# A graph network on one core: the merge of an item's rows moves into the next step

## The chip, the cores and the metric

The kernel runs on one core of one Trainium2 chip. The metric is the device time of one execution in microseconds (us); the time of a kernel is the median of several executions.

## What is computed

A graph has 6250 nodes and 206250 edges sorted by destination node. Three attention layers (GATv2) run over it, then a layer norm, then a node model that uses sums of the edge attributes, then another layer norm. Cut to what matters here, one layer is:

```python
e_feat = leaky_relu(xl[src] + xr[dst])            # xl = h @ Wl + bl, xr = h @ Wr + br
logits = einsum('ehc,hc->eh', e_feat, att)
m      = segment_max(logits, dst)                 # per destination node and head
a      = exp(logits - m[dst]); denom = segment_sum(a, dst)
h      = segment_sum(xl[src] * a / denom[dst], dst) + bias
h      = relu(layer_norm(h) * g + be)             # input of the next layer
```

The node model also needs `segment_sum(edge_attr, dst)` and a count per node; the kernel takes both in its first layer.

## The kernel before, in words

Edges are cut into chunks of 3328 (26 tiles of 128), and a chunk with its window of 128 destination nodes is an **item**: 62 items in each of three **stages** (one stage per attention layer). All engines run the same software pipeline, written out by hand in `pipeline` (L450) as a chain of **steps**. A step *opens* one item, *closes* the item opened a step earlier, and *begins* the next one (its preparation). In stages 0 and 1 it also *turns* an item closed earlier: it makes that window's rows of the next layer's tables.

The 26 tiles are handled in 7 groups, six of four tiles and one of two. For an opened item, per group:

- GpSimd gathers the rows `xl[src]` by one indirect DMA per tile (L706). It may be two groups ahead of VectorE and no more: before group g it waits for the z of group g-2 (L701), and for groups 0 and 1 for the last two groups of the item before (L703).
- ScalarE builds one-hot matrices: `S` (edge by node, `onehot`, L906 and L909) and its transpose `ST` (`onehotT`, L931 and L936).
- TensorE spreads the node rows `xr` over the edges with `ST` (`expand`, L763; groups 0 and 1 of an item are made at the end of the step before, L812).
- VectorE adds both parts, which is z (`add_transforms`, L1186), and takes the logits (`relu_att` L1193, `sum_heads` L1202 or L1205, `add_linear` L1216).

For a closed item VectorE finds the running maxima over segments (`runs`, `carries`, `maxima`), subtracts them (`shift`, L1275), ScalarE takes the exponentials (L953), VectorE weights the gathered rows (`message`, L1285), and TensorE sums them by node into one PSUM bank (`sums`, L791; in stage 0 also the edge attributes, `attribute_sums`, L783, with a clearing product L778 ahead). Then comes the **merge** with the state of that window in memory: `new_max` (L1294 to L1304), an exponential on ScalarE (`rescale`, L966), `new_state` (L1311 to L1320). In stages 0 and 1 `turn_norm` (L1328 to L1344, 15 dependent small operations) normalizes the merged rows; TensorE transposes and multiplies them (`turn_rows` L743, `turn_products` L748 and L749), ScalarE copies (L885, L894, L896), VectorE takes their logits (`turn_logits`, L1352 to L1361).

In the kernel before, VectorE does `new_max` in the last group of the step that closes the item, and `new_state` and `turn_norm` behind that group, at the end of the step. The next step begins with `runs`, and only then comes its first z. SyncE loads items and stores rows in a fixed order (`item_step`, L605): it waits for the merge, stores the window, waits for the store, and loads the next window.

Each engine runs its own list in order, so a waiting instruction holds everything behind it.

## Time and profile before

| | |
|---|---|
| median of 3 executions | 8529.99 us (8517.47 to 8535.05) |
| the profiled execution | 8491.84 us, span 8489.9 us |
| busy: TensorE, VectorE, ScalarE, GpSimd | 4879.8, 5222.4, 4307.0, 4740.8 us |
| mean granted TensorE clock | 0.679 of full speed |
| moved by DMA | 697.83 MB, mean 82 GB/s |

The profiled execution is 0.45% below the median. The span runs from the first to the last instruction. No engine is busy for more than 62% of it.

### The profile page before, as it was taken

To read this page: it belongs to the slowest core of one execution; us is meant where nothing else is said; L and a number is where in the kernel's file an instruction comes from. 1 tells how busy PE (TensorE), PEld (TensorE's weight loads), DVE (VectorE), ACT (ScalarE), POOL (GpSimd) and SP (SyncE) were. 2 spreads that over 40 slices of the span, in tenths; PEclk is the share of its full clock that TensorE was granted. 3 is DMA by queue.
4 is the path that set the end of the run, shared out by engine and by line. 5 is a ranking of instruction groups with operands and counts; after the bars stand their busy time and mean duration, and the time that the engine had idled before them with its cause. 6 is when DMAs were issued, how large, how long until landed. Compare 5 with 4: busy or idle time off the path is not lost.

```text
span 8489.9 us, 109176 instructions
## 1 busy us (share of the span) xinstructions
PE 4879.8 (57%) x24176; PEld 4286.7 (50%) x24176; DVE 5222.4 (62%) x16308; ACT 4307.0 (51%) x10681; POOL 4740.8 (56%) x4843
## 2 busy tenths in 40 slices
PE   4666666666666655555555555545555555544446
PEld 3565656565656544444444444444444444444444
DVE  5555565656565656766666667655555555555556
ACT  3444444444454545555555555545555555555546
POOL 3555555555555545666666666656666666666640
PEclk7666666666666666766767767666666666666666
DMA  5333333333333322322322323222222222222221
GB/s 147 94 100 91 96 97 97 97 96 97 96 98 95 98 67 74 79 76 76 77 75 77 82 77 78 76 66 72 77 71 71 72 72 72 76 73 72 72 61 50
DMA packets 460163, 697.83 MB, mean 82 GB/s; under 512 B 140781, under 2 KB 330019, under 8 KB 460101
## 3 DMA queue, kind: packets, MB, share of 16 engines
q0 software_dynamic: 154752, 327.15, 16.9%
q1 hardware_dynamic: 305349, 370.00, 14.2%
q8 instruction: 21, 0.34, 0.0%
q14 instruction: 41, 0.34, 0.0%
HBM read 638.95 MB, written 57.76 MB: 82 GB/s over the span
## 4 chain that ended last, share of the span: by engine, by line
PE 33%; issue 27%; DVE 22%; another core or an unknown queue 7%; ACT 6%; POOL 3%; DMA 2%; SPq 0%; DVEq 0%; ACTq 0%; POOLq 0%
PE PS L791 14%; PE PS L763 10%; PE PS L783 6%; DVE z L1186 3%; POOL xl_g L706 3%; DVE am L1193 3%; DVE msg L1285 2%; ACT distT L931 2%; ACT ST L936 2%; DVE relu_logit L1202 1%; ACT dist L906 1%; PE PS L749 1%; DMA xl_g<-xl_tab,edges 1%; DVE relu_logit L1205 1%
## 5 line engine op out<-in xcount | busy, mean ns | idle before, releaser
L706 POOL DMA_INDIRECT xl_g<-xl_tab,edges x4836 | 4740.0, 980 | 3485.8 <-DVE z L1186 1689.1
L763 PE MATMUL PS<-xr_w,ST 128*128 128x132 f32 x9672 | 2054.2, 373 | 2160.7 <-issue 1278.8
L763 PEld LDWEIGHTS PS<-xr_w,ST 128*128 128x128 f32 x9672 | 1778.9, 269 | 2455.4 <-issue 1735.2
L791 PE MATMUL PS<-msg,S 128*128 128x137 f32 x9672 | 1829.7, 352 | 936.8 <-issue 648.7
L791 PEld LDWEIGHTS PS<-msg,S 128*128 128x128 f32 x9672 | 1710.6, 257 | 1017.6 <-issue 1012.0
L1186 DVE TENSOR_TENSOR z<-PS,xl_g 128x528 f32<-128x528 f32 x1302 | 856.6, 658 | 1428.1 <-DMA xl_g<-xl_tab,edges 823.2
L906 ACT ACTIVATE dist<-node_row,neg_dst 128x128 f32<-128x128 f32 x4836 | 1534.5, 386 | 0.0
L931 ACT ACTIVATE distT<-dst_all,neg_node 128x512 f32<-128x512 int16 x1302 | 884.0, 679 | 1029.7 <-DVE neg_dst L1179 725.5
L909 ACT ACTIVATE S<-dist 128x512 f32<-128x512 f32 x1302 | 780.4, 599 | 839.9 <-remote 625.2
L1193 DVE SCALAR_TENSOR_TENSOR am<-z,att_relu 128x512 f32<-128x512 f32 x1302 | 860.8, 661 | 115.0 <-remote 94.1
L936 ACT ACTIVATE ST<-distT 128x512 f32<-128x512 f32 x1302 | 780.0, 599 | 42.6 <-ACT distT L931 1.4
L1285 DVE TENSOR_TENSOR msg<-xl_g,msg 128x512 f32<-128x512 f32 x1302 | 792.8, 644 | 0.2 <-ACT msg L953 0.2
L783 PE MATMUL PS<-ea,S 128*128 128x96 f32 x3224 | 628.6, 366 | 194.3 <-issue 194.1
L783 PEld LDWEIGHTS PS<-ea,S 128*128 128x128 f32 x3224 | 593.1, 278 | 260.3 <-issue 260.0
L1202 DVE TENSOR_REDUCE relu_logit<-am 128x16 f32<-128x512 f32 x868 | 557.0, 642 | 30.6 <-DVE am L1193 11.1
L1294 DVE TENSOR_SCALAR some<-PS 128x1 f32<-128x1 f32 x186 | 29.5, 158 | 836.2 <-PE PS L791 578.2
L966 ACT ACTIVATE rescale<-dmax 128x8 f32<-128x8 f32 x186 | 38.8, 208 | 879.0 <-DVE dmax L1304 802.1
L953 ACT ACTIVATE msg<-shifted 128x104 f32<-128x104 f32 x186 | 56.7, 305 | 716.0 <-issue 522.7
L1205 DVE TENSOR_REDUCE relu_logit<-am 128x4 f32<-128x512 f32 x434 | 278.3, 641 | 22.7 <-DVE am L1193 11.9
L1216 DVE TENSOR_TENSOR logit<-relu_logit,z 128x16 f32<-128x16 f32 x1302 | 227.5, 175 | 93.0 <-remote 82.1
L1243 DVE TENSOR_TENSOR_SCAN run_up<-row_pen,PS 128x128 f32<-128x128 f32 x186 | 77.8, 418 | 175.0 <-PE PS L770 98.7
L894 ACT COPY t_lr<-PS 128x264 f32<-128x264 f32 x124 | 46.9, 378 | 246.1 <-PE PS L749 168.7
(220 smaller groups left out, 3691.4 us busy)
## 6 DMA issues: line engine op xcount, KB each, us to landing
dst_all<-dst_short SPq DMA_DIRECT2D x186, 832.0 KB
xl_g<-xl_tab,edges POOLq DMA_INDIRECT x4836
ea<-edge_attr SPq DMA_DIRECT2D x124, 432.0 KB
ea<-edge_attr SPq DMA_DIRECT2D x62, 384.0 KB
xr_w<-xr_tab SPq DMA_DIRECT2D x186, 66.0 KB
dst_r<-dst_rows SPq DMA_DIRECT2D x186, 64.0 KB
node_row<-node_id SPq DMA_DIRECT2D x186, 64.0 KB
state<-t_new SPq DMA_DIRECT2D x126, 68.0 KB
```

What stands on the lines that cost most here:

```text
L706: pool.indirect_dma_start(xl_g[:, q, t, :], None, xl_tab[stage][:, :], bass.IndirectOffsetOnAxis(idx[:, q, t:t + 1], 0))\
L763: last = pe.matmul(zp[(q + g) % 3][:, n, :], ST[:, t, :], xr_w[:, q, :], start=True, stop=True)
L783: last = pe.matmul(ea_ps, S[:, q, t, :], ea[:, q, t, :], start=False, stop=False)
L791: last = pe.matmul(agg_ps, S[:, q, t, :], msg[:, t, :], start=t == 0 and stage > 0, stop=t == TILES - 1)
L906: last = act.activation(dist[:, (q + g) % 2, m, :], node_row[:, q, :], ACT.Abs, bias=neg_dst[:, q, t:t + 1])
L909: act.activation(S[:, q, GROUPS[g][0]:GROUPS[g][0] + n, :], dist[:, (q + g) % 2, 0:n, :], ACT.Relu, bias=1.0, scale=-1.0)\
L931: act.activation(distT[:, (q + g) % 2, 0:n], dst_all[:, q, GROUPS[g][0] * P:GROUPS[g][0] * P + n], ACT.Abs, bias=neg_node[:, q:q + 1]).the ...
L936: act.activation(ST[:, GROUPS[g][0]:GROUPS[g][-1] + 1, :].rearrange("p t n -> p (t n)"), distT[:, (q + g) % 2, 0:n], ACT.Relu, bias=1.0, s ...
L1186: dve.tensor_tensor(out=z[:, (q + g) % 2, 0:n, :], in0=zp[(q + g) % 3][:, 0:n, :], in1=xl_g[:, q, a:a + n, :], op=ALU.add).then_inc(z_done ...
L1193: dve.scalar_tensor_tensor(am[:, (q + g) % 2, 0:n, :], z[:, (q + g) % 2, 0:n, 0:F], 0.0, att_relu[:, stage, :].unsqueeze(1).to_broadcast([ ...
L1202: s = dve.reduce_sum(relu_logit[:, a * HEADS:(a + n) * HEADS], am[:, (q + g) % 2, 0:n, :].rearrange("p t (h f) -> p (t h) f", h=HEADS), ax ...
L1285: dve.tensor_tensor(out=msg[:, a:a + n, 0:F].rearrange("p t (h f) -> p t h f", h=HEADS), in0=xl_g[:, q, a:a + n, 0:F].rearrange("p t (h f) ...
```

## The change

The argument `turned` of a step becomes `merges`: the item that was closed one step earlier, in all three stages (the last stage gets one more step at its end for that). Merge and normalization of an item now run in the step after the one that closes it:

- VectorE: a step begins with the z of group 0, then `new_max` of the item merged, then `runs` of the item closed. `new_state` stands behind the z of group 1, `turn_norm` at the end of group 1, `turn_logits` in group 5 (it was in group 2).
- ScalarE: `rescale` stands behind the first one-hot of the step; the two turning copies and the exponentials of the closed item trade places.
- TensorE: `turn_rows` and `turn_products` go from groups 0 and 1 to groups 2 and 3. Ahead of the sums TensorE waits, as before, for the copy that frees the bank, and in the last stage for the merge (`item_done`).
- SyncE: the state of item k-1 is stored, and that of item k loaded, behind the loads for item k+2; the turned rows are stored behind the attribute loads.

```diff
                     for g in range(NG):
                         if opens and g + 2 < NG:
                             expand(opens, g + 2)
-                        if turned and g < 2:
-                            (turn_rows, turn_products)[g]()
                         if closes and g == 2:
                             close("max")
+                        if turned and g in (2, 3):
+                            (turn_rows, turn_products)[g - 2]()
                         if turned and closes and g == 3:
                             pe.wait_ge(n_copied, turned[1] + BLOCKS)
+                        elif merges and closes and g == 3:
+                            pe.wait_ge(item_done, merges[1])
...
                     if opens:
                         onehotT(opens, 2)
+                    if merges:
+                        rescales()
+                    if opens:
                         onehot(0)
+                        onehotT(opens, 3)
+                        onehot(1)
+                        onehotT(opens, 4)
                     if turned:
                         turn_hidden()
+                    if closes:
+                        alphas()
                     if opens:
-                        onehotT(opens, 3)
-                        onehot(1)
+                        onehotT(opens, 5)
+                        onehot(2)
                     if turned:
                         turn_copies()
...
                 for g in range(NG):
-                    if closes and g == 0:
-                        runs()
-                    if closes and g == 1:
-                        carries()
                     if opens:
                         add_transforms(g)
                         if g:
                             add_linear(g - 1)
+                    if merges and g == 1:
+                        new_state()
+                    if closes and g == 1:
+                        carries()
                     if closes and g == 2:
                         shift()
-                    if turned and g == 2:
+                    if turned and g == 5:
                         turn_logits()
                     if opens:
                         relu_att(g)
+                    if merges and g == 0:
+                        new_max()
...
                         sum_heads(g)
-                    if closes and g == NG - 1:
-                        new_max()
+                    if closes and g == 0:
+                        runs()
+                    if turned and g == 1:
+                        turn_norm()
...
                 if opens:
                     add_linear(NG - 1)
-                if closes:
-                    new_state()
-                    if stage < LAYERS - 1:
-                        turn_norm()
...
                 def item_step(k, q, behind):
-                    here, ahead = window(k), window(k + 1)
...
                     load_item(k + 2, q, stage)
-                    if turns and behind:
-                        store_turned(k - 1, stage, before)
+                    if behind:
+                        store_merged(k, q)
...
+                    if turns and behind:
+                        store_turned(k - 1, stage, before)
```

**VectorE, the head of a step in stage 0, before.** `t_norm` ends the normalization; `run_up` and `run_down` are `runs`; `z`, `am`, `relu_logit` are group 0.

```order
L1344 TENSOR_SCALAR t_norm<-t_y,t_mv,t_rstd 128x128
L1243 SCALAR_TENSOR_TENSOR run_up<-row_pen,PS 128x128
L1244 SCALAR_TENSOR_TENSOR run_down<-row_pen,PS 128x128
L1186 TENSOR_TENSOR z<-PS,xl_g 128x528
L1193 SCALAR_TENSOR_TENSOR am<-z,att_relu 128x512
L1202 TENSOR_REDUCE relu_logit<-am 128x16
L1251 STREAM_TRANSPOSE run_T<-run_up 128x32
```

The same place now, from the z of group 0 to the z of group 1; `some` to `dmax` is `new_max`.

```order
L1205 TENSOR_TENSOR z<-PS,xl_g 128x528
L1212 SCALAR_TENSOR_TENSOR am<-z,att_relu 128x512
L1313 TENSOR_SCALAR some<-PS 128x1
L1315 TENSOR_SCALAR none_pen<-some 128x1
L1317 TENSOR_SCALAR chunk_max<-PS,none_pen 128x4
L1320 TENSOR_TENSOR st_new<-chunk_max,st_old 128x4
L1322 TENSOR_TENSOR dmax<-st_old,st_new 128x4
L1323 TENSOR_TENSOR dmax<-chunk_max,st_new 128x4
L1221 TENSOR_REDUCE relu_logit<-am 128x16
L1262 SCALAR_TENSOR_TENSOR run_up<-row_pen,PS 128x128
L1263 SCALAR_TENSOR_TENSOR run_down<-row_pen,PS 128x128
L1205 TENSOR_TENSOR z<-PS,xl_g 128x528
```

The z of group 0 now stands ahead of the merge and of `runs`.

**VectorE, ahead of the z of group 2 in stage 0, before** (`up` and `seg_max` are `maxima`, `shifted` is `shift`):

```order
L1267 SCALAR_TENSOR_TENSOR up<-row_pen,carry_T,PS 128x128
L1269 SCALAR_TENSOR_TENSOR seg_max<-row_pen,carry_T,up 128x128
L1202 TENSOR_REDUCE relu_logit<-am 128x16
L1186 TENSOR_TENSOR z<-PS,xl_g 128x528
L1216 TENSOR_TENSOR logit<-relu_logit,z 128x4x4
L1275 TENSOR_TENSOR shifted<-logit,PS 128x104
```

And now, with the last operations of `turn_norm` ahead of it:

```order
L1361 SCALAR_TENSOR_TENSOR t_newton<-t_rstd,t_half 128x1
L1362 SCALAR_TENSOR_TENSOR t_rstd<-t_newton,t_rstd 128x1
L1363 TENSOR_SCALAR t_norm<-t_y,t_mv,t_rstd 128x128
L1205 TENSOR_TENSOR z<-PS,xl_g 128x528
L1235 TENSOR_TENSOR logit<-relu_logit,z 128x4x4
L1294 TENSOR_TENSOR shifted<-logit,PS 128x104
```

The whole normalization has moved from ahead of the first z to ahead of the third.

**TensorE, a step of stage 0 from the transposed logits (`L770`) to the first attribute sums (`L783`), before:**

```order
L770 MATMUL PS<-ident,logit 128x128
L763 MATMUL PS<-xr_w,ST 128x132 x4
L743 MATMUL PS<-ident,t_norm 128x128
L763 MATMUL PS<-xr_w,ST 128x132 x4
L748 MATMUL PS<-b_parts,ones_h 128x264
L749 MATMUL PS<-w_lr,t_hT 128x264
L763 MATMUL PS<-xr_w,ST 128x132 x4
L773 MATMUL PS<-ident,seg_max 128x128
L763 MATMUL PS<-xr_w,ST 128x132 x4
L778 MATMUL PS<-zeros,ones 128x233
L783 MATMUL PS<-ea,S 128x96 x9
```

And now:

```order
L774 MATMUL PS<-ident,logit 128x128
L767 MATMUL PS<-xr_w,ST 128x132 x12
L777 MATMUL PS<-ident,seg_max 128x128
L747 MATMUL PS<-ident,t_norm 128x128
L767 MATMUL PS<-xr_w,ST 128x132 x4
L752 MATMUL PS<-b_parts,ones_h 128x264
L753 MATMUL PS<-w_lr,t_hT 128x264
L782 MATMUL PS<-zeros,ones 128x233
L787 MATMUL PS<-ea,S 128x96 x9
```

The two turning products now stand directly ahead of the sums.

## Rows read from the trace of the kernel before

**Rows 1.** The page: busy us (share of the span) and instructions of each engine
```profile
PE 4879.8 (57%) x24176; PEld 4286.7 (50%) x24176; DVE 5222.4 (62%) x16308; ACT 4307.0 (51%) x10681; POOL 4740.8 (56%) x4843
```
**Rows 2.** Line L1294 in stage 0, 1 and 2: duration ns, first and last start
```profile
L1294 DVE TENSOR_SCALAR some<-PS x62: 157/158/160, 194.1 to 3065.6; 128x1 f32<-128x1 f32 x62
...
L1294 DVE TENSOR_SCALAR some<-PS x62: 157/159/160, 3165.0 to 5668.9; 128x1 f32<-128x1 f32 x62
...
L1294 DVE TENSOR_SCALAR some<-PS x62: 157/159/160, 5767.0 to 8249.4; 128x1 f32<-128x1 f32 x62
```
**Rows 3.** Timeline, VectorE, a stage 0 step: start us, us, operation [idle before <-releaser]
```profile
2003.31 0.16 DVE L1294 TENSOR_SCALAR some<-PS 128x1 f32<-128x1 f32 x1 [9.63 <-PE PS L791]
...
2004.75 0.29 DVE L1311 TENSOR_TENSOR scaled<-st_old,rescale 128x128 f32<-128x128 f32 x1 [0.19 <-ACT rescale L966]
...
2005.85 0.18 DVE L1328 RECIPROCAL t_rd<-st_new 128x4 f32<-128x4 f32 x1
...
2009.74 0.41 DVE L1243 TENSOR_TENSOR_SCAN run_up<-row_pen,PS 128x128 f32<-128x128 f32 x1
...
2010.38 0.68 DVE L1186 TENSOR_TENSOR z<-PS,xl_g 128x528 f32<-128x528 f32 x1
...
2015.97 0.65 DVE L1202 TENSOR_REDUCE relu_logit<-am 128x16 f32<-128x512 f32 x1
...
2028.22 0.71 DVE L1186 TENSOR_TENSOR z<-PS,xl_g 128x528 f32<-128x528 f32 x1 [0.81 <-DMA xl_g<-xl_tab,edges]
...
2056.94 0.68 DVE L1186 TENSOR_TENSOR z<-PS,xl_g 128x528 f32<-128x528 f32 x1
```
**Rows 4.** Timeline, TensorE, the same step
```profile
2014.16 0.40 PE L748 MATMUL PS<-b_parts,ones_h 3*128 3x264 bf16 x1
...
2024.22 2.13 PE L763 MATMUL PS<-xr_w,ST 128*128 128x132 f32 x8 [3.85 <-issue]
...
2027.35 4.16 PE L783 MATMUL PS<-ea,S 128*128 128x96 f32 x18
...
2049.40 0.80 PE L763 MATMUL PS<-xr_w,ST 128*128 128x132 f32 x5 [0.19 <-issue]
```
**Rows 5.** Timeline, ScalarE, the same step
```profile
2015.99 0.38 ACT L894 COPY t_lr<-PS 128x264 f32<-128x264 f32 x1 [2.18 <-PE PS L749]
...
2022.80 0.70 ACT L931 ACTIVATE distT<-dst_all,neg_node 128x512 f32<-128x512 int16 x1
```
**Rows 6.** Timeline, GpSimd, the same step
```profile
2011.85 0.94 POOL L706 DMA_INDIRECT xl_g<-xl_tab,edges  x1 [13.65 <-DVE z L1186]
```
**Rows 7.** Line L706, GpSimd, whole span: duration ns min/median/max
```profile
L706 POOL DMA_INDIRECT xl_g<-xl_tab,edges x4836: 938/944/1487, 102.4 to 8226.3; - x194
```
**Rows 8.** Timeline, VectorE, a stage 1 step
```profile
4513.68 0.71 DVE L1186 TENSOR_TENSOR z<-PS,xl_g 128x528 f32<-128x528 f32 x1 [2.34 <-issue]
...
4514.85 0.28 DVE L1352 TENSOR_TENSOR t_sum<-t_lr 128x128 f32<-128x128 f32 x1
...
4516.09 0.69 DVE L1193 SCALAR_TENSOR_TENSOR am<-z,att_relu 128x512 f32<-128x512 f32 x1
...
4528.70 0.71 DVE L1186 TENSOR_TENSOR z<-PS,xl_g 128x528 f32<-128x528 f32 x1 [0.63 <-DMA xl_g<-xl_tab,edges]
...
4532.04 0.69 DVE L1193 SCALAR_TENSOR_TENSOR am<-z,att_relu 128x512 f32<-128x512 f32 x1 [2.54 <-remote]
...
4534.30 0.43 DVE L1186 TENSOR_TENSOR z<-PS,xl_g 128x264 f32<-128x264 f32 x1
```
**Rows 9.** Timeline, ScalarE, the same stage 1 step
```profile
4514.80 0.30 ACT L953 ACTIVATE msg<-shifted 128x104 f32<-128x104 f32 x1 [2.18 <-issue]
```
**Rows 10.** Timeline, TensorE, the same stage 1 step
```profile
4536.82 1.17 PE L763 MATMUL PS<-xr_w,ST 128*128 128x132 f32 x8 [0.81 <-issue]
```
**Rows 11.** Timeline, a stage 2 step: GpSimd, then VectorE
```profile
7011.61 0.94 POOL L706 DMA_INDIRECT xl_g<-xl_tab,edges  x1 [4.34 <-DVE z L1186]
...
7042.90 0.43 DVE L1186 TENSOR_TENSOR z<-PS,xl_g 128x264 f32<-128x264 f32 x1 [5.75 <-remote]
```

More of the change, by code:

```diff
@@ L455, in item @@
                 return q, pairs * (2 * stage) + 2 * i + (q + 1), pairs * stage + i + 1
-            def turned(i, q):
-                return item(i, q) if stage < LAYERS - 1 else None
             step(None, None, item(0, 0), None)
@@ L603, in _, with store_merged, logits_made @@
                 sp.dma_start(st_old[:, 0, 0:ROW if first else ROW_L], state[stage][bass.ds(windows[0], P), :]).then_inc(state_loaded[0], 16)
-                def item_step(k, q, behind):
-                    here, ahead = window(k), window(k + 1)
+                width = ROW if first else ROW_L
+                def store_merged(k, q):
+                    here, ahead = window(k - 1), window(k)
+                    sp.sem_inc(spacer, 1)
+                    sp.wait_ge(item_done, before + k)
+                    sp.dma_start(state[stage][bass.ds(here, P), :], st_new[:, 1 - q, 0:width]).then_inc(state_stored, 16)
+                    sp.wait_ge(state_stored, (before + k) * 16)
+                    sp.dma_start(st_old[:, q, 0:width], state[stage][bass.ds(ahead, P), :]).then_inc(state_loaded[q], 16)
+                def logits_made(k):
                     sp.wait_ge(onehot_done[NG - 1], (before + k + 1) * 2)
@@ L736, in _, with pe_step @@
             for stage in range(LAYERS):
-                def pe_step(opens, closes, begins, turned):
+                def pe_step(opens, closes, begins, merges):
+                    turned = merges if stage < LAYERS - 1 else None
                     def turn_rows():
@@ L879, in _, with act_step @@
             for stage in range(LAYERS):
-                def act_step(opens, closes, begins, turned):
+                def act_step(opens, closes, begins, merges):
+                    turned = merges if stage < LAYERS - 1 else None
                     def turn_hidden():
@@ L1042, in _ @@
             ch = Chain(dve, setup)
+            dve.sem_inc(merge_step, 4)
             for g in range(NG):
@@ L1170, in node_logits, with edge_step @@
                 assert n.n == LOGIT_STEPS, n.n
-            def edge_step(stage, opens, closes, begins, turned):
+            def edge_step(stage, opens, closes, begins, merges):
+                turned = merges if stage < LAYERS - 1 else None
                 def prepare():
@@ L1417, in _ @@
             for stage in range(LAYERS):
-                pipeline(dve, stage, pairs, last_pair, lambda opens, closes, begins, turned: edge_step(stage, opens, closes, begins, turned))
+                pipeline(dve, stage, pairs, last_pair, lambda opens, closes, begins, merges: edge_step(stage, opens, closes, begins, merges))
             dve.wait_ge(hid_bias, 1)
```

85 lines of the change are left out of this document (38 added, 47 removed).

## The prediction

> **What bounds the kernel now.** I read the page first. No engine is near its span: VectorE is busy 5222.4 us of 8489.9, GpSimd 4740.8, TensorE 4879.8 [rows 1]. So the time is not an engine's work but a loop of waits. Next, the line that opens the merge, stage by stage. It runs 62 times in each, so 61 steps lie between its first and last start [rows 2]: (3065.6-194.1)/61 = 47.1 us a step in stage 0, 41.05 in stage 1, 40.7 in stage 2. That makes 61 x 128.8 = 7860 of the 8490 us; the rest is set-up, stage ends and the node model, which the change leaves alone.
>
> Then the timeline of one step of stage 0. The merge starts at 2003.31, after VectorE stood idle 9.63 us for TensorE's sums; merge, normalization and `runs` take until 2010.38, and only there stands the first z [rows 3]. GpSimd, which may gather only two groups ahead of z, had been idle 13.65 us and starts 0.8 us behind that z [rows 6]. Everything later in the step follows from it. In stage 0 TensorE starts its long run of sums at 2027.35 and is through with it and with the spread of the next item's group 0 at 2049.40+0.80 = 2050.20 [rows 4]. The next z comes at 2056.94 [rows 3]. So the loop is: z, sums start (17.0 us later), sums and spread end (22.85), merge chain until the next z (6.7): 46.6 us, close to the mean of 47.1. In stages 1 and 2 the same loop holds, with the gathers as its middle part: the GpSimd waits there are 4.34 us in the stage 2 step shown [rows 11].
>
> **The change, part by part.** It adds and removes next to no work: the same operations on other places. What counts is what each place holds up.
>
> *(a) The first z no longer waits for merge, normalization and `runs`.* It still waits for the spread of group 0, which TensorE, in order, does behind the sums. In stage 0 it can come 0.15 us behind 2050.20 in place of 2056.94: -6.6 us a step.
>
> *(b) The same VectorE work now lies between z of group 0 and z of group 2.* Before, from z at 2010.38 to the end of the group 1 reduction at 2015.97+0.65, VectorE ran without a gap: 6.2 us. To it comes 2003.31 to 2010.38, 7.07 us, less 0.19 of waiting and 0.17 for the last group's `add_linear` that lies inside [rows 3]: 6.7. So z of group 2 can start 12.9 us behind the first z. (Without the normalization, 2005.85 to 2009.74, it is 9.0.)
>
> *(c) The turning products now stand right ahead of the sums.* From z of group 2: exponentials done after 4514.80+0.20-4513.68 = 1.3 us [rows 8, 9]; the transposed one-hot of group 5, 2022.80 to TensorE's start at 2024.22, 1.4 [rows 4, 5]; its spread, 2.1; the two products and the copy, 2014.16 to 2015.99+0.38, 2.2 [rows 4, 5]; then 1.0 from the end of the spread at 2026.35 to the first attribute sum, with the clearing product [rows 4]. 12.9+1.3+1.4+2.1+2.2+1.0 = 20.9, with hand-overs 21.0, against 17.0: +4.0 us a step in stage 0.
>
> *Stage 0*: 21.0+22.85+0.15 = 44.0 against 46.56: -2.5 us. x 61 = **-153 us**. ScalarE's last S one-hots, now behind the copy, are covered by the 22.85 us of sums, which begin with attributes.
>
> *Stage 1*, no attribute sums, so the gathers set the middle. GpSimd may start group 4 when z of group 2 is done: 12.9+0.7+0.8 = 14.4. In the stage 0 step group 4's z came at 2028.22, 16.4 us behind GpSimd's start of group 2 at 2011.85 [rows 3, 6], less two groups of four at 0.944+0.30 us each [rows 7] (10.0): 6.4 from a group's start to its z. One group later, +5.1: z of group 5 at 25.9. To z of group 6, 4534.30-4528.70 = 5.6, plus `turn_logits`, which moved in there, 1.25 (4514.85 to 4516.09): 6.85 [rows 8]. From there to the next first z: one-hot and spread of group 0, which began 4536.82-4534.30 = 2.5 later and took 1.2 [rows 8, 10], and I take 0.5 for sums still ahead of it on TensorE: 4.2. Sum 37.0; the shown steps are shorter than the mean (46.6 against 47.1), so 37.8 against 41.05: -3.2 us. x 61 = **-195 us**.
>
> *Stage 2*, no normalization: z of group 2 at 9.0 is not late for the gathers. GpSimd's wait for the first z, 4.34 us, shrinks to the usual 0.30 [rows 11]: -4.0. Against that stands contention. With two SBUF operands on VectorE beside them, gathers grew from 0.944 to as much as 1.487 us [rows 7]; the merge has some four such operations that used to run while GpSimd waited. Between nothing and 4 x 0.54 = 2.2 I take 0.3, since the mean gather is near its median. -3.7 x 61 = **-226 us**.
>
> On that point the Trainium skill, "GPSIMD Engine Reference", section 1 (Specifications), says that GpSimd shares its SBUF interfaces with VectorE and contends with VectorE instructions that have two SBUF inputs. The rule speaks against this change; by it at its full price stage 2 would gain 1.8 us a step in place of 3.7. The trace agrees that some gathers are longer, up to 1.487 us, and does not say by which operation.
>
> *SyncE*: the item loads no longer wait for the merge in stages 1 and 2, so their burst comes some 3 us earlier and may meet the gathers of groups 0 and 1. No row shows it there; bounds 0 and +2 us a step, taken as 0, since in the stage 1 step, with the burst right ahead of it, VectorE waited no more than 2.34 us for the gather of group 2 [rows 8]. State store and load have a whole step of slack: nothing. *Stage ends*: the last merge waited for the last sums before and does so now: nothing, at worst 5 us each.
>
> Sum: -574 us. The profiled execution of 8491.8 becomes 7918; it stood 0.45% below the median of 8530, so the forecast is **7950 us**.
>
> **The rivals.**
>
> *R1, faster than forecast.* Late in a step all engines stand still without a releaser that the trace names: 2.54 us in the stage 1 step [rows 8], 5.75 us in the stage 2 step [rows 11]. I carried these over. If they belong to the old arrangement, stages 1 and 2 come down to the gathers' floor: 26 x 1.3+0.8 = 34.6 in stage 2 (-6.1), 35.6 in stage 1 (-5.4), and stage 0, where TensorE's sums hold such a stall too, to -5.2. That is -1020 us: 7510. For it: nothing in the program asks for the stalls. Against: they stand in nearly every step.
>
> *R2, a third of the gain.* Burst and contention at their upper ends (+2 and +1.9 a step in stages 1 and 2), stage 0 -1.5: -1.5, -1.2, -1: some -225 us, 8300.
>
> *R3, slower.* TensorE takes its list in order. In stages 0 and 1 it now holds sums, and behind them the next item's spread and so the next first z, until ScalarE's copy of the turned rows is done; that copy was 11 us early before (2016.37 against 2027.35 [rows 4, 5]) and is the last thing to come now. It decides once the copy comes 4.7 us later than 19.9 us behind the first z (574/122 steps). If a late-step stall (up to 5.75 us) falls ahead of it, both stages lose: 122 x 5.75-574 = +128 us, 8660. For it: the products run on a TensorE that has just waited. Against: the stall shown stood behind the z of group 5 [rows 8], not ahead.
>
> *R4, it doesn't do what it says.* If the first z waits for something else by the same amount (the gather of group 0, say), (a) is empty and (b), (c) nearly so: 8530. Against: GpSimd had stood idle for 13.65 us ahead of its group 2 [rows 6], so groups 0 and 1 had long been issued.
>
> **How the numbers follow.** Forecast 0.56, R1 0.17, R2 0.17, R3 0.06, R4 0.04. Cases that leave the range: half of R1's far end, R3, R4. The range is 7580 to 8370 us. A measurement tells 0.2%, some 17 us, from no change: faster 0.90, within 0.03, slower 0.07.
>
> **What would show it.** Right: L1313 of the new profile spaced 44 to 45 us in stage 0, about 38 in stage 1, 37 in stage 2; GpSimd's long idle ahead of group 2 gone and, in stages 0 and 1, a shorter one ahead of group 4; z of group 2 some 13 us behind the first z, 9 in stage 2; the first attribute sum 21 us behind it, released by the copy L902. Wrong: a step of stage 0 over 47 us; TensorE waiting for L902 past 25 us; steps of stage 1 or 2 under 36 us, which would be R1; GpSimd's mean gather over 1.05 us, which would be R2.

## The result and the profile after

| | before | changed | ratio, 95% interval |
|---|---|---|---|
| the timed pair | 8529.99 us | 8574.09 us (8559.03 to 8581.07) | 1.0058 [1.0046, 1.0069] |
| the same pair again, in a later session (e7) | 8473.16 us | 8301.36 us (8286.34 to 8309.03) | 0.9799 [0.9781, 0.9816] |

The change made the kernel 0.6% slower where 6.8% faster was forecast. Run again in another session it was 2% faster. (A session, named a call in the expectations below, stands for kernels timed together on one chip, beside fresh runs of before. The five later sessions each had another chip; that of the first pair is not on record.) So there are two questions: why the gain is small everywhere, and why its sign changes.

The line that opens the merge, stage by stage, first timed pair, changed kernel (against [rows 2]):

```profile
L1313 DVE TENSOR_SCALAR some<-PS x62: 150/151/159, 200.3 to 2974.9; 128x1 f32<-128x1 f32 x62
...
L1313 DVE TENSOR_SCALAR some<-PS x62: 150/151/159, 3082.4 to 5741.0; 128x1 f32<-128x1 f32 x62
...
L1313 DVE TENSOR_SCALAR some<-PS x62: 150/152/159, 5848.6 to 8317.2; 128x1 f32<-128x1 f32 x62
```

Divided by 61: 45.5, 43.6 and 40.5 us a step, against 47.1, 41.05 and 40.7. Stage 0 gained 97 us, stage 1 lost 155, stage 2 gained 14, and what lies between and around the stages cost 23: +67 us, the difference of the spans (8557.0 and 8489.9). So the loss is in stage 1. One of its steps, all engines, in order of time (start us, us, operation, idle before and releaser):

```profile
4537.25 0.71 DVE L1205 TENSOR_TENSOR z<-PS,xl_g 128x528 f32<-128x528 f32 x1 [7.82 <-PE PS L767]
...
4551.17 0.70 DVE L1205 TENSOR_TENSOR z<-PS,xl_g 128x528 f32<-128x528 f32 x1
...
4552.68 1.10 POOL L708 DMA_INDIRECT xl_g<-xl_tab,edges  x1 [3.80 <-DVE z L1205]
...
4558.35 2.16 PE L795 MATMUL PS<-msg,S 128*128 128x137 f32 x8 [0.88 <-issue]
...
4567.89 1.02 DVE L1304 TENSOR_TENSOR msg<-xl_g,msg 128x512 f32<-128x512 f32 x2
...
4568.71 0.72 PE L795 MATMUL PS<-msg,S 128*128 128x137 f32 x4 [0.83 <-issue]
4568.82 0.42 DVE L1205 TENSOR_TENSOR z<-PS,xl_g 128x264 f32<-128x264 f32 x1
...
4571.97 0.28 PE L795 MATMUL PS<-msg,S 128*128 128x137 f32 x1 [2.54 <-issue]
...
4572.68 0.42 DVE L1221 TENSOR_REDUCE relu_logit<-am 128x8 f32<-128x256 f32 x1 [2.18 <-issue]
...
4574.78 0.39 PE L795 MATMUL PS<-msg,S 128*128 128x137 f32 x1 [2.53 <-issue]
4574.80 0.72 ACT L939 ACTIVATE distT<-dst_all,neg_node 128x512 f32<-128x512 int16 x1 [8.04 <-remote]
4575.15 0.94 POOL L708 DMA_INDIRECT xl_g<-xl_tab,edges  x1 [0.30 <-issue]
...
4576.88 0.39 PE L795 MATMUL PS<-msg,S 128*128 128x137 f32 x1 [1.71 <-issue]
...
4578.30 1.49 PE L795 MATMUL PS<-msg,S 128*128 128x137 f32 x5 [1.04 <-issue]
...
4581.59 0.71 DVE L1205 TENSOR_TENSOR z<-PS,xl_g 128x528 f32<-128x528 f32 x1 [5.22 <-PE PS L767]
```

z of group 2 comes 13.9 us behind the first z (forecast 12.9), z of group 6 31.6 us behind it (32.8). Up to here it is within 1.2 us of the forecast. But from there to the next first z it takes 12.8 us, where 4.2 were forecast. The last messages are there at 4568.9; TensorE then does its last sums one by one with 1 to 2.5 us between them, and VectorE and ScalarE stand still beside it. GpSimd alone keeps its pace. Its chain of 18 indirect DMAs began at 4552.68 (the longest pause in it is 0.67 us), TensorE stops some 17 us into it, the last DMA of the step ends at 4576.09, and 2 us later everybody runs again.

TensorE's weight loads stand still as well. By their event records the two that start at 4573.38 and 4576.17 neither wait for a semaphore nor update one:

```profile
4573.38 0.29 PEld L795 LDWEIGHTS PS<-msg,S 128*128 128x128 f32 x1 [2.65 <-issue]
4576.17 0.29 PEld L795 LDWEIGHTS PS<-msg,S 128*128 128x128 f32 x1 [2.50 <-issue]
```

The stall was there before, in the stage 1 step of [rows 8]. GpSimd's chain of 18 began at 4506.64 and ended at 4529.53; ScalarE stops 17 us into it, between `dist` operations that are done and the `S` that needs nothing else:

```profile
4506.64 0.94 POOL L706 DMA_INDIRECT xl_g<-xl_tab,edges  x1 [4.06 <-DVE z L1186]
...
4526.44 0.63 ACT L909 ACTIVATE S<-dist 128x512 f32<-128x512 f32 x1 [2.56 <-remote]
```

VectorE's 2.54 us of [rows 8] end 2.5 us behind that chain. So it is this late-step stall, grown. In all of stage 1, TensorE's idle time in front of the sums:

```profile
L795 PE MATMUL PS<-msg,S 128*128 128x137 f32 x3172 | 665.9, 369 | 549.4 <-issue 546.5 <-ACT t_lr L902 1.7 <-DVE msg L1304 1.0
```

That is 546.5/61 = 9.0 us a step in which it waited for nothing that the trace names. Some 0.9 of them stand at the first sum (4558.35), which follows ScalarE's copy L902 (done at 4558.11), and are no stall.

One more thing changed beside it: the mean granted TensorE clock of stage 1 was 0.69 before and 0.63 now, and TensorE's busy time a step rose from 22.6 to 24.6 us. The mean sum took 369 ns in both. How much of the 2.0 us lies on the path was not tested.

### The profile page after: what moved, and what is told of

Read it like the earlier page. It is cut to its first block, busy times and chain, and to the rows that moved or that the text cites. A ratio compares the mean times of both kernels' runs of the same rounds, so it can differ in the third digit from the quotient of the medians.

```text
span 8557.0 us, 109590 instructions
## 1 busy us (share of the span) xinstructions
PE 4961.6 (58%) x24176; PEld 4337.0 (51%) x24176; DVE 5109.9 (60%) x16308; ACT 4305.5 (50%) x10681; POOL 4791.0 (56%) x4843
## 4 chain that ended last, share of the span: by engine, by line
PE 33%; DVE 30%; issue 23%; another core or an unknown queue 8%; ACT 4%; DMA 1%; POOL 1%; DVEq 1%; SPq 0%; ACTq 0%; POOLq 0%
PE PS L795 16%; PE PS L767 7%; PE PS L787 6%; DVE z L1205 5%; DVE am L1212 3%; DVE msg L1304 2%; PE PS L753 2%; ACT distT L939 1%; DVE t_newton L1361 1%; ACT ST L944 1%; DVE t_bits L1358 1%; DVE relu_logit L1221 1%; DVE t_rstd L1362 1%; DVE relu_logit L1224 1%
## 5 line engine op out<-in xcount | busy, mean ns | idle before, releaser
L708 POOL DMA_INDIRECT xl_g<-xl_tab,edges x4836 | 4790.2, 991 | 3506.1 <-issue 1774.1
L767 PE MATMUL PS<-xr_w,ST 128*128 128x132 f32 x9672 | 2144.0, 389 | 1945.3 <-ACT ST L944 1099.4
L767 PEld LDWEIGHTS PS<-xr_w,ST 128*128 128x128 f32 x9672 | 1886.6, 285 | 2175.0 <-issue 1605.0
L795 PE MATMUL PS<-msg,S 128*128 128x137 f32 x9672 | 1850.7, 351 | 1016.8 <-issue 949.5
L1212 DVE SCALAR_TENSOR_TENSOR am<-z,att_relu 128x512 f32<-128x512 f32 x1302 | 841.0, 646 | 10.0 <-DVE z L1205 2.3
L787 PE MATMUL PS<-ea,S 128*128 128x96 f32 x3224 | 548.0, 339 | 39.5 <-issue 39.2
L787 PEld LDWEIGHTS PS<-ea,S 128*128 128x128 f32 x3224 | 528.3, 255 | 58.5 <-issue 58.1
L893 ACT ACTIVATE t_hT<-PS,be_col,g_col 128x128 f32<-128x128 f32 x124 | 56.7, 457 | 737.2 <-PE PS L747 737.2
L747 PE MATMUL PS<-ident,t_norm 128*128 128x128 f32 x124 | 59.0, 475 | 380.6 <-DVE t_norm L1363 380.6
L1294 DVE TENSOR_TENSOR shifted<-logit,PS 128x104 f32<-128x104 f32 x186 | 60.5, 325 | 316.3 <-remote 298.7
```

Of the source, the lines that this page charges most:

```text
L708: pool.indirect_dma_start(xl_g[:, q, t, :], None, xl_tab[stage][:, :], bass.IndirectOffsetOnAxis(idx[:, q, t:t + 1], 0))\
L767: last = pe.matmul(zp[(q + g) % 3][:, n, :], ST[:, t, :], xr_w[:, q, :], start=True, stop=True)
L787: last = pe.matmul(ea_ps, S[:, q, t, :], ea[:, q, t, :], start=False, stop=False)
L795: last = pe.matmul(agg_ps, S[:, q, t, :], msg[:, t, :], start=t == 0 and stage > 0, stop=t == TILES - 1)
L1212: dve.scalar_tensor_tensor(am[:, (q + g) % 2, 0:n, :], z[:, (q + g) % 2, 0:n, 0:F], 0.0, att_relu[:, stage, :].unsqueeze(1).to_broadcast([ ...
```

## The experiments

"Us a step" is the spacing of the merge's first line. The expectations count from z to z in the middle of a stage, which gives some 0.5 us more (44.2 where the table has 43.6). For stage 1, "sum gaps" is the idle time in front of the sums by issue, as in the row above. The kernels of the first four later sessions (e1 to e4, e5 to e8, e9 to e12, e13 to e16) ran beside runs of before at 8459 to 8475 us, those of the last (e17, e18) at 8521. Where one execution alone was taken, its time stands in place of a ratio.

| kernel | us a step, stages 0, 1, 2 | sum gaps, us a step | ratio |
|---|---|---|---|
| before, first trace | 47.1, 41.05, 40.7 | | 1 |
| changed, first trace | 45.5, 43.6, 40.5 | 9.0 | 1.0058 |
| e12 before | 46.8, 40.7, 40.7 | 2.5, and 3.1 remote | 1 |
| e7 changed | 44.0, 41.8, 39.6 | 8.3 | 0.980 |
| e1 half the gathers | 44.0, 31.4, 28.6 | 0 | 6917 us |
| e2 small item load | 44.0, 42.0, 39.8 | 8.3 | 8323 us |
| e5 narrow rows | 43.9, 41.8, 39.9 | 8.6 | 8314 us |
| e6 plain DMAs | 44.05, 31.1, 28.0 | 0 | 6866 us |
| e9 pause for z of group 6 | 42.9, 45.4, 40.3 | 0.9 | 1.001 |
| e10 pause for the sums | 44.0, 46.2, 39.9 | 0.9 | 8590 us |
| e13 pauses ahead of groups 2, 4, 6 | 43.7, 41.3, 41.1 | 0.3 | 0.985 |
| e14 before, same pauses | 43.6, 41.85, 41.7 | 2.7 | 0.990 |
| e15 pause ahead of each | 48.2, 47.9, 48.3 | | 9506 us |
| e16 64 more instructions | 46.9, 46.6, 47.45 | 4.4 | 9247 us |
| e3 spread first | 44.7, 41.5, 40.2 | | 0.987 |
| e4 change in stage 0 | 44.05, 40.6, 40.9 | | 0.9815 |
| e8 the same, spread first | 44.5, 40.6, 40.7 | | 0.984 |
| e11 change in stages 0 and 2 | 44.0, 40.7, 40.3 | | 0.971 |
| e17 two pauses | 44.3, 43.4, 39.9 | | 0.990 |
| e18 e11 and e9's wait in stage 0 | 44.2, 41.3, 40.3 | | 0.980 |

**What the stall needs: e1, e2, e5, e6.**

```diff
-for t in tiles:
+for t in tiles[::2] if stage else tiles:
```


> The changed kernel, but in stages 1 and 2 only every second tile of a group is gathered (13 indirect DMAs an item in place of 26); VectorE works on old rows for the others, so this part of the computation is left out there. Stage 0 is unchanged. In the changed kernel a step of stage 1 takes 44.2 us, and between 32 and 42 us behind its first z TensorE does single sums with 1 to 2.5 us between them though its operands are ready: 7 to 9 us a step. Theory G (the stall comes from GpSimd's gathers when they run without a pause): the gaps in the sums shrink below 2 us a step and stage 1 falls to 35 us or less. Theory L (the stall comes from the item load): gaps stay at 7 us, a step takes about 42 us. Theory I (instruction supply that has nothing to do with either): also stays. My forecast's own sum, with no gathers in the way, gives about 33 us for stage 1.

```diff
-dst_all[:, q, :], dst_short[bass.ds(ch, 1), :]
+dst_all[:, q, 0:wide], dst_short[bass.ds(ch, 1), 0:wide]     # wide = P if stage else CHUNK
```


> The changed kernel, but in stages 1 and 2 the broadcast of an item's destinations to all partitions loads 128 columns in place of 3328 (0.03 MB in place of 0.85 MB); the one-hots there use old destinations, so this part of the computation is left out. Theory L (the item load causes the late stall): gaps in the sums of stage 1 fall from 8 to under 2 us, a step from 44.2 to about 37. Theory G and theory I: stage 1 stays at 43 to 44.5 us, the gaps at 7 us or more.

```diff
-pool.indirect_dma_start(xl_g[:, q, t, :], None, xl_tab[stage][:, :], ...)
+pool.indirect_dma_start(xl_g[:, q, t, 0:wide], None, rows[:, :], ...)     # wide = 33 in stages 1 and 2
```


> The changed kernel, but in stages 1 and 2 each of the 26 indirect DMAs of an item fetches 33 numbers a row in place of 132: as many DMAs and rows, a quarter of the bytes; rows are other ones and the rest of each row is old, so this part is left out. With half the DMAs (e1) the stall was gone and a step of stage 1 took 31.6 us. If the bytes matter (the transfer engines are the shared resource): the stall goes, stage 1 takes 35 to 38 us, the gathers' floor. If the number of rows and GpSimd's work on them matter: the stall stays, stage 1 at 42 to 44 us.

```diff
+else:
+    pool.dma_start(xl_g[:, q, t, :], xl_tab[stage][t * P:(t + 1) * P, :]).then_inc(gathered[q][g], 16)
```


> The changed kernel, but in stages 1 and 2 GpSimd fetches each tile by a plain DMA of 128 consecutive rows in place of an indirect one: as many DMAs and the same bytes, no indices; rows are other ones, so this part is left out. If what stalls the engines is GpSimd's work on the indices: the stall goes, stage 1 takes 34 to 37 us or less. If it is the transfers or the number of DMAs: stage 1 stays at 42 to 44 us.

The sums in stage 1 of e1, e2, e5 and e6, each from its own trace (busy us, mean ns, idle before):

```profile
L795 PE MATMUL PS<-msg,S 128*128 128x137 f32 x3172 | 544.0, 344 | 53.2 <-ACT t_lr L902 53.2
```
```profile
L796 PE MATMUL PS<-msg,S 128*128 128x137 f32 x3172 | 639.6, 360 | 515.8 <-issue 503.9 <-ACT t_lr L903 8.7 <-DVE msg L1305 2.1
```
```profile
L796 PE MATMUL PS<-msg,S 128*128 128x137 f32 x3171 | 647.1, 364 | 541.3 <-issue 526.0 <-ACT t_lr L903 11.3 <-DVE msg L1305 3.6
```
```profile
L798 PE MATMUL PS<-msg,S 128*128 128x137 f32 x3172 | 538.3, 341 | 53.1 <-ACT t_lr L905 53.1
```

A twenty-sixth of the load's columns and a quarter of the gathers' bytes change nothing: theory L and the bytes are out. Half the indirect DMAs, or plain DMAs of the same bytes, take the gaps to zero and a step of stage 1 to 31 us. So the stall of the three other engines comes with GpSimd's indirect DMAs at their full rate. Whether plain DMAs could bring it on is open: e6's occupy GpSimd for 535 ns in place of 944, and no chain of them was longer than 10, or 6.1 us. e1's longest was 5 us.

**How they do it: e9, e10, e13, e15.**

```diff
-pool.wait_ge(z_done[NG + g - BEHIND], ...)
+pool.wait_ge(z_done[NG - 1], ...)
```


> The changed kernel, in which GpSimd waits ahead of groups 0 and 1 of the next item for the z of the last group (it waited for that of the last but one for group 0): a pause of some 4 us in the chain of indirect DMAs of a step, nothing else. e1 and e6 showed that the stall of the other engines comes with the indirect DMAs, at a full rate for 17 us or more. If a pause lets the others recover: the gaps in the sums of stage 1 (8 us a step) fall to 3 us or less, the first z is then held by the gather of group 0, some 41 us behind the last first z, and stage 1 goes from 42.3 to 41 or less; ratio 0.5 to 1% under the changed kernel's 0.980. If the number of indirect DMAs in a step decides: no change in the gaps, the later gathers only add, ratio 0.980 to 0.99.

Both branches of that were wrong for stage 1. The gaps did leave the sums (the 0.9 us that are left are the wait for the copy), yet the step grew to 45.4 us. VectorE in a stage 1 step of e9:

```profile
4164.28 0.18 DVE L1235 TENSOR_TENSOR logit<-relu_logit,z 128x16 f32<-128x16 f32 x1
...
4167.02 0.21 DVE L1273 TENSOR_TENSOR_SCAN open_max<-through_pen,run_T 128x26 f32<-128x26 f32 x1 [1.49 <-issue]
...
4169.83 0.19 DVE L1277 TENSOR_TENSOR carry<-open_max,enter_pen 128x26 f32<-128x26 f32 x1 [2.50 <-remote]
...
4172.62 0.25 DVE L1280 STREAM_TRANSPOSE carry_T<-carry 128x64 f32<-128x64 f32 x1 [2.50 <-issue]
```

and GpSimd, where the chain starts and where it ends:

```profile
4151.44 0.95 POOL L708 DMA_INDIRECT xl_g<-xl_tab,edges  x1 [4.58 <-DVE z L1205]
...
4160.20 0.95 POOL L708 DMA_INDIRECT xl_g<-xl_tab,edges  x1 [0.30 <-issue]
...
4170.27 0.94 POOL L708 DMA_INDIRECT xl_g<-xl_tab,edges  x1 [0.30 <-issue]
```

The later gathers of groups 0 and 1 now run into those of groups 2 and 3 without a pause, 16 DMAs or 20 us, and the stall stands 14 us into that chain, on small VectorE operations that need nothing from DMA. In the changed kernel's step above it stood some 17 us behind 4552.68. The stall goes with the chain, not with the place in the program. In stage 0 e9's pauses break the chain, and a step fell from 44.0 to 42.9 us.

```diff
+if stage == 1 and g == 0:
+    pool.wait_ge(agg_done, ...)     # the last sums of the item being closed
```


> The changed kernel, but in stage 1 GpSimd starts the gathers of the next item only when TensorE has done the last sums of the item being closed, so that no indirect DMA runs beside the end of the sums. If the stall needs indirect DMAs beside the stalled work: no gaps in the last sums, which end some 33 us behind the first z (40 in e7); the next first z then waits for a gather, 33+8 = 41 us. If the stall is owed to what went before in the step (a store that has run empty, say), the gaps stay and a step of stage 1 takes 48 us or more.

As e9: the long gaps in the sums are gone, and the stall stands in `carries`, 16 to 20 us into a chain of 16 (46.2 us a step). Step and gaps together fit neither branch: the first had left out where the stall would go.

```diff
+if g in PAUSES:     # (2, 4, 6); each of 1 to 6 in e15
+    pool.wait_ge(gathered[q][g - 1], (pairs * stage + i + 1) * (16 * len(GROUPS[g - 1])))
```


> The changed kernel, in which GpSimd waits ahead of groups 2, 4 and 6 until the rows of the group before have landed (some 2 us each). No unbroken chain of indirect DMAs is then longer than 10 (12.6 us; it was 18 or more, 23 us and over). As many DMAs as before. If an unbroken chain of some 16 us is what brings the stall: no gaps in the sums of stage 1, which is then held by GpSimd at 26 x 1.25+3 x 2 = 38.5 to 39.5 us (42.3), stage 2 at 38.5 to 39 (40.2), stage 0 at 43.3 (44.4): 250 to 370 us less than the changed kernel, ratio 0.936 to 0.951. If the number of DMAs decides: the pauses only cost, 0.98 to 1.01.

> As e13, with a pause ahead of each of groups 1 to 6, so that no chain is longer than 6. If chains of 10 are short enough, there is nothing left to win and the pauses cost: 26 x 1.25+6 x 2 = 44.5 us a step in stages 1 and 2, and no stall in any. If a stall was left in e13 and is gone here, the chain must be shorter than 10.

The sums of stage 1 in e13:

```profile
L799 PE MATMUL PS<-msg,S 128*128 128x137 f32 x3172 | 623.1, 368 | 257.7 <-DVE msg L1308 188.4 <-ACT t_lr L906 49.0 <-issue 20.3
```

and GpSimd's pauses in one of its steps:

```profile
4090.95 0.94 POOL L712 DMA_INDIRECT xl_g<-xl_tab,edges  x1 [2.58 <-issue]
...
4103.69 1.35 POOL L712 DMA_INDIRECT xl_g<-xl_tab,edges  x1 [2.58 <-DMA xl_g<-xl_tab,edges]
...
4116.65 0.94 POOL L712 DMA_INDIRECT xl_g<-xl_tab,edges  x1 [2.56 <-DMA xl_g<-xl_tab,edges]
```

As many indirect DMAs, but none of the chains longer than 10, and the 8.3 us of gaps became 0.3. That settles what the gaps follow: the unbroken chain. It also brings the late part of the step near its forecast: from z of group 6 to the next first z stage 1 now takes 5.5 us in the mean, with all 26 gathers (12.5 in the first trace of the changed kernel, 4.2 forecast). A rest is left at the end of the one chain of 10 (4116.65 to 4129.43 in this step), on VectorE, 54 times in stage 1 and 105.7 us in all (1.7 a step):

```profile
4131.04 0.42 DVE L1266 TENSOR_TENSOR_SCAN run_up<-row_pen,PS 128x128 f32<-128x128 f32 x1 [2.00 <-remote]
```

That is 12.4 us into the chain and until 1.6 us behind it. In e15, with chains of 6 at most, no such wait stands on VectorE.

The time did not follow: three pauses of 2.6 us put GpSimd on the path, and 41.3 us a step is little less than 41.8. The expectation of 38.5 to 39.5 had GpSimd's list too short: its DMAs took 1.004 us in the mean here, so 26 x (1.004+0.30)+3 x (2.6-0.30) = 40.8. e15, with six pauses, came out at 47.9 against an expected 44.5 in the same way (26 x (1.012+0.30)+6 x 2.3 = 47.9).

**The kernel before with the same pauses: e14.**


> The kernel before with the same pauses as in e13. Its chain from group 2 to group 1 of the next item is 28 DMAs, 36 us. If the chain brings the stall: the waits of 3 to 5 us a step go, but the pauses ahead of groups 4 and 6 lie on the path from first z to last: net 0 to -1.5 us a step in stages 1 and 2, ratio 0.98 to 1.0. The distance of e13 to e14 is then what the change is worth without stalls; my forecast's terms make it 2.5 to 3.7 us a step.

8387.56 us, 0.9897 [0.9875, 0.9919]: stage 0 fell by 3.1 us a step, more than by the change itself, stages 1 and 2 rose by 1. Against e13 (0.9848 [0.9824, 0.9871]) the change is worth half a per cent where both have their pauses, not 2.5 to 3.7 us a step. In stages 1 and 2 GpSimd is then near its bound in both: beyond its pauses of 2.6 us and its 0.30 between DMAs it idles 0.6 to 1.8 us a step.

Two numbers need a word. The chain of 28 in the expectation can't be: an item has 26 gathers, and in the stage 1 step of before shown above the chain is 18. And the 2.7 us of sum gaps in e14 are no stall: in the step at 3112 TensorE starts 0.1 us behind the end of the message that it waits for, a wait of 4.30 us which the profile puts down to issue.

**Instructions: e16.**

```diff
+if opens and g == 1:
+    for _ in range(64):
+        pe.sem_inc(spacer, 1)
```


> The changed kernel with 64 semaphore increments that nobody waits for, on TensorE, behind the spread of group 3, where TensorE has time (its first 15 us of a step are half idle). The loop's instructions on TensorE grow by a third to a half. If the stall is an instruction supply that runs low while GpSimd works without a pause, it comes earlier or grows: the gaps in the sums of stage 1 go from 8 us to 11 or more, stage 1 to 45. If it has nothing to do with the number of instructions: 42.3 us, as in e7, or 1 us over it where the increments themselves delay.

TensorE, then GpSimd, in a stage 2 step (the increments have no rows; they stand in the idle time of 13.27 us):

```profile
7028.65 2.12 PE L767 MATMUL PS<-xr_w,ST 128*128 128x132 f32 x8 [4.32 <-ACT ST L947]
7044.04 2.10 PE L767 MATMUL PS<-xr_w,ST 128*128 128x132 f32 x8 [13.27 <-issue]
```
```profile
7024.07 0.95 POOL L708 DMA_INDIRECT xl_g<-xl_tab,edges  x1 [3.73 <-DVE z L1208]
...
7038.27 0.95 POOL L708 DMA_INDIRECT xl_g<-xl_tab,edges  x1 [0.30 <-issue]
```

By the trace's event records the increments come every 0.15 us at first. From about the 22nd on, 8 us into GpSimd's chain (at 7032.1 here), they come singly or in pairs, 0.7 us apart. In stages 0 and 1, where the chain ends soon, that lasts for some five of them; in stage 2 until 7041 in this step, 2 us behind the chain's last DMA. They wait for nothing and touch no data, so operands and their ports are out for them; the two weight loads above touch no semaphore, so a slow semaphore alone is out for those. What both have in common is that they have to be issued. That points to the supply of instructions as what runs short beside a long chain. It is an inference: no run saw the supply itself. A denser list ran short earlier, 8 us into the chain in place of 12 to 17; since the increments always begin 4.5 to 4.8 us into it, the run can't tell whether the time in the chain or the number of instructions decides. The expected growth of the gaps in the sums did not come (4.4 us): GpSimd had then been held up ahead of group 5, which broke its chain.

The Trainium skill, "Runtime: NRT & Kernel Launch", section "Instruction fetch mechanics", says that each engine fetches its instructions in blocks over a DMA queue of its own and that this is mostly hidden. If the supply is what runs short here, it is not hidden. But the changed kernel's profile shows only 64 packets on its two instruction queues in a run of 186 steps (68 in e16), so no run here shows by which route the loops' instructions come, or what they wait for:

```profile
q8 instruction: 21, 0.34, 0.0%
q14 instruction: 43, 0.34, 0.0%
```

**The two sessions: e7 and e12.**


> The changed kernel again, unaltered, on the chip of this call, so that the others have their base here. Ratio 1.0046 to 1.0069 as at first if chips don't matter; the kernel of before took 8459 us in the call before this one and 8530 at first, so ratios may differ by some tenths of a per cent.

> The kernel before, unaltered, for its trace on the chip of this call. Its first trace had steps of 47.5, 41.5 and 41.2 us. Since its median was 8530 at first and 8459 and 8473 in the later calls, 60 us less: if that is spread evenly, 47.2, 41.1, 40.9 us. The changed kernel lost 272 us between the calls (8574 to 8301), so chips differ in something that hurts the changed order more; in its first trace the normalization took about a microsecond more and the sums of stage 1 more gaps.

Changed kernel (e7), then before (e12):

```profile
L1313 DVE TENSOR_SCALAR some<-PS x62: 150/151/159, 194.9 to 2878.0; 128x1 f32<-128x1 f32 x62
...
L1313 DVE TENSOR_SCALAR some<-PS x62: 150/152/158, 2984.6 to 5531.9; 128x1 f32<-128x1 f32 x62
...
L1313 DVE TENSOR_SCALAR some<-PS x62: 150/151/159, 5638.6 to 8054.7; 128x1 f32<-128x1 f32 x62
```
```profile
L1294 DVE TENSOR_SCALAR some<-PS x62: 157/159/160, 195.6 to 3048.4; 128x1 f32<-128x1 f32 x62
...
L1294 DVE TENSOR_SCALAR some<-PS x62: 157/159/160, 3151.9 to 5634.3; 128x1 f32<-128x1 f32 x62
...
L1294 DVE TENSOR_SCALAR some<-PS x62: 157/159/159, 5733.8 to 8214.2; 128x1 f32<-128x1 f32 x62
```

These two traces are from two sessions, too, in which before took 8473 and 8475 us. Here the change gave 170 us in stage 0, lost 65 in stage 1 and gave 64 in stage 2. Against the first traces, the steps of before are shorter by 0.3, 0.4 and 0.0 us, those of the changed kernel by 1.5, 1.8 and 0.9. Most of what differs is waiting ahead of z of group 2: in the first trace of the changed kernel it came 14.6 us behind the first z in stage 0 and 14.0 in stage 1, with waits inside the normalization's small operations (0.3 to 0.6 us each in the stage 1 step above), and 13.5 and 12.8 us in e7. In stage 1 the sum gaps add 0.7. GpSimd's DMAs took as long in both (mean 991 and 987 ns). Why one session stalls more than the other was not found. That the changed order feels it more because it keeps more dependent work beside GpSimd's chains would fit, and was not tested.

**Versions: e3, e4, e8, e11, e17, e18.**

e3 moves `expand(begins, 0)` and `expand(begins, 1)` ahead of the last two groups of sums:

```diff
+if begins and g == NG - 1:
+    expand(begins, 0)
+    expand(begins, 1)
 if closes:
     for m in SUMS_AT.get(g - 1, ()):
         sums(m)
-if begins:
-    expand(begins, 0)
-    expand(begins, 1)
```


> The changed kernel, with TensorE's spread of groups 0 and 1 of the next item ahead of the last two groups of sums in place of behind them. In the changed kernel VectorE waits 7 to 8 us a step in stage 1 for that spread, because it is queued behind sums that stall. If that queueing is what costs: the first z comes about 8 us earlier in stage 1, but the merge that stands behind it on VectorE still waits for the sums, so 1 to 2 us a step net in stage 1 and in stage 0: -120 to -240 us, ratio to the kernel before 0.975 to 0.99. If the stall simply moves along (all engines stop, whatever TensorE's order): no change, 1.005.

0.987 [0.9853, 0.9888], in the expected band but 0.7% above e7, so no gain: the expectation had its base from the first pair. Against e7 stage 1 gained 0.3 us a step, stages 0 and 2 lost 0.7 and 0.6. The changed kernel was not timed in e3's session, but e2, whose small load changed nothing, took 8323 us there and e3 8353.

e4, e8 and e11 choose the order by stage (`LATE = (0,)`, or `(0, 2)`; the others run as before), e8 with e3's edit in stage 0:

> The change in stage 0 only; stages 1 and 2 run in the order of before. Step lengths in the traces: stage 0 46.0 against 47.5, stage 1 44.2 against 41.5, stage 2 41.1 against 41.2. If the stages don't act on each other: 61 x -1.5 = -92 us against before, ratio 0.989. If the gain of stage 0 was a matter of one profiled execution: 1.000.

> e4 (the change in stage 0 only, 0.9815) with e3's edit added in that stage: the spread of the next item ahead of the last two groups of sums. e3's stage 0 step was 45.1 against 46.0 of the changed kernel's first profile, but 44.5 in e4's. If the spread held the loop: -0.9 us a step, another -55 us, ratio 0.975. If the merge behind the first z waits for the sums anyway: as e4, 0.9815.

> The change in stages 0 and 2, stage 1 in the order of before. By step lengths on the chip of e4 and e7: stage 0 44.4 (changed) against about 47, stage 1 40.95 (before) against 42.3 (changed), stage 2 40.2 (changed) against 41.3 (before). So 61 x 1.3 = 80 us under the changed kernel: 8220 us, ratio 0.971 where the changed kernel has 0.980.

e4: 0.9815 [0.9799, 0.9832]. e8: 0.9842 [0.9826, 0.9859], in another session and with overlapping intervals: no gain, where 55 us were expected. e11: 8231.63 us, **0.9707 [0.9680, 0.9733]**, the fastest. Its ratio is the expected one, its trace less so: the traced execution took 8271 us, the slowest of four, and stage 2 in it 40.3 us a step where e7 had 39.6. The changed kernel was not timed in that session, but e10, altered in stage 1 alone, had 44.0 and 39.9 us there in stages 0 and 2. What e11 has over it is stage 1: 40.7 us, as before, for the 41.8 of e7. In e4 and e11 every stage comes within 0.4 us of what its order takes in the traces of before (e12) and changed (e10), so the stages can be chosen one by one.

e17 puts pauses ahead of groups 2 and 5 in stages 1 and 2 and e9's wait in stage 0; e18 is e11 with that wait in stage 0:

> The changed kernel with two forced pauses a step in stages 1 and 2, ahead of groups 2 and 5 (chains of 12 and 14 indirect DMAs, 15 and 17.5 us), and in stage 0 the wait for the last z of e9 in their place. GpSimd then needs 26 x 1.25+2 x 2.6+0.7 = 38.4 us a step, and in stage 1 some 1 us for z of group 2. If chains of 14 are short enough: stage 1 at 39.5, stage 2 at 39, stage 0 at 43.3: 311 us under the changed kernel's 8301, 7990 us, ratio 0.943. If a stall of 2 us or more is left in such chains: stages 1 and 2 at 41 to 42, ratio 0.97 to 0.98.

> e11 (the change in stages 0 and 2; ratio 0.9707) with e9's wait in stage 0: GpSimd starts groups 0 and 1 of the next item only behind the last z. Stage 0 was 43.3 us a step in e9 and 44.5 in e11: 61 x -1.1 = -67 us, ratio 0.963. If e9's gain in stage 0 was the other way about (it came from chance): 0.971.

0.9902 [0.9886, 0.9919] and 0.9804 [0.9783, 0.9826], beside a before of 8521 us, near the 8530 of the first pair, in which the changed kernel had 1.0058. Stage 1 of e17 took 43.4 us, and its first z came 9.7 us behind z of group 6 (4.4 in e1): the stall fell behind the spreads of the next item, some 17 us into the chain of 14. Such a chain is still too long, and the pauses cost. Whether e18 beats e11 stays open, as e11 was not timed in that session. That e18, with the change in stages 0 and 2, is 2% faster than before there is shown; that the whole change would not have been is likely from the first pair and was not timed. In stage 0 both took 44.2 to 44.3 us, 1.2 less than the 45.5 of the first pair, as e9 took 1.1 less than e7.

## Why the prediction was wrong

- **Forecast 7950, range 7580 to 8370, measured 8574.** The sign was wrong in the first pair; in the later one it was right, with a third of the gain. That 8301 is R2's 8300 is luck: R2 had it from burst and contention, and e2 and the mean gather speak against both.
- **(a) right.** The first z no longer waits for merge and normalization; it waits for the spread (7.82 us <-PE in the step above).
- **(b) 12.9 us to z of group 2**: measured 14.6 and 14.0 in stages 0 and 1 of the first trace, 13.5 and 12.8 in e7, 12.3 in stage 1 of e1 without stalls. The term was right for a VectorE that is not held up.
- **(c) sums at 21.0 us**: the first attribute sum came at 22.6 in the first trace (21.6 in e7), with the clearing product 0.05 us behind the copy L902, as forecast; from there to the next first z it was 23.4 (22.8 in e7), where 23.0 was forecast. So stage 0 gained 1.6 us in the first trace and 2.8 in e7, where 2.5 was forecast.
- **Stage 1, the step that failed**: "From there to the next first z ... 4.2", with the remark in R1 that the late-step stalls were "carried over". In the mean of 55 steps it is 4.4 with the gathers halved (e1), 5.5 with all of them in chains of at most 10 (e13), and 12.5 with full chains (11.8 in e7). The stall was taken as a constant of the step. In truth it follows GpSimd's unbroken chain: from some 12 to 17 us into it the other engines stand still for most of the time until it ends. Before, the chain of 18 began behind the first z and stalled the last groups. Now it begins behind z of group 2, and the sums start 21.2 us behind the first z (15.6 before), so that their end and the next spread, on which the next first z waits, lie in the last third of the chain.
- **Stage 2, -3.7 us**: 0.2 in the first trace, 1.0 in e7. The term that failed is GpSimd's wait for the first z, 4.34 that "shrinks to the usual 0.30". It did not: in the mean GpSimd idled 4.2 us ahead of group 2 before and 4.1 after (4.0 in e12, 3.3 in e7). The first z no longer waits for the merge, but it came 10.7 us behind z of group 6 (8.9 in e7), for the same reason as in stage 1: in e13 that stretch is 5.1 and in e1 4.4. With half the gathers the step takes 28.6 us, so no other engine was in the way.
- **R1** had the stall right as the thing to doubt and the sign wrong: it could grow, and no rival said so. **R3** had the right place, TensorE's queue with the next spread behind the sums, but the stall fell on the sums and not ahead of the copy. **R4** is out: the first z moved. GpSimd's mean gather went from 980 to 991 ns, which speaks against R2's size for contention. That some contention is there would fit this: in the changed kernel's trace 1180 of 4836 gathers took over 1.0 us, and beside these VectorE's `am` and `msg`, which have two SBUF operands, ran 477 ns in the mean, beside the others 117.
- **Stage ends** and what lies around the stages: 23 us, forecast nothing, at worst 5 for each end (8.5 in e7 against e12).
- **Slips in the sums**, too small to matter: 37.0 us scaled by 47.1/46.6 is 37.4 and not 37.8; the exponential in (c) has 0.20 where its row shows 0.30; R2's terms make stage 2 -3.7+1.9+2 = +0.2 and not -1, some 8380 us in all.

## What to carry to other kernels

An idle time without a releaser is not a constant that can be carried into the new schedule: find out what it follows, by halving or pausing each engine that keeps running through it, before a price is put on anything that moves beside it. Where GpSimd issues indirect DMAs back to back for more than some 12 us, as here, put critical work at the beginning of the chain or let the chain break where a wait is free; pauses put in by force cost as much as they gave (e13, e15, e17). When a change helps in one stage and harms in another, apply it by stage, and time such a kernel in more than one session.

## What was not expected of the hardware

- Beside an unbroken chain of indirect DMAs on GpSimd (944 ns each, 0.30 us between) TensorE, VectorE and ScalarE came nearly to a stop: 12 us into it in e13, 14 in e9, 17 in the traces of before and changed and in e17, 8 in e16 with its 64 increments. Single instructions then came 1 to 2.5 us apart until 1 to 2.5 us behind the chain's end. A chain of 10 (12.8 us) brought one wait of 2 us at its end, chains of 14 and more brought 4 us and over. A pause of 2.6 us ended it, one of 0.67 us did not.
- It is neither bytes (a quarter of them: same) nor the number of DMAs (the same number with pauses: gone). Plain DMAs from GpSimd, 535 ns each, did not bring it on in chains of up to 6.1 us; longer ones were not run.
- Semaphore increments on TensorE, which need no data, went from 0.15 us apart to one or two every 0.7 us beside the chain; in the changed kernel weight loads that touch no semaphore stood still for 2.5 us, too.
- The same two kernels differed by +0.6% in one session and by -2.0% in another, with intervals 0.2 to 0.4% wide.
